# A graph layer with counted slots: longer runs of tiles with a slot range per tile, and row masks by fours

## The chip, the core and the metric

The kernel runs on one core of one Trainium2 chip. Time is device time in microseconds (us) of a whole execution. The engines are PE (matrix products), DVE (VectorE), ACT (ScalarE), POOL (GpSimd) and SP (queues of transfers); each has its own instruction list and they meet at semaphores.

## The reference

Features of 3125 nodes are normalised. 100,000 edges (src, dst, relation), sorted by dst, take the message of their source node, which is a two-layer network with the weights of the edge's relation; the messages are summed by dst. A gated unit and three small layers follow, then a routed feed-forward part for the best half of the nodes. dst is drawn as 3125 u², so low nodes have many more edges.

```
msgs = where(rel == r, relu(relu(S @ W[r].T + b[r]) @ W[r].T + b[r]))   # S = feat[src]
agg = segment_sum(msgs, dst)
gates = agg @ W_ih.T + b_ih + b_hh;  i, f, g, o = split(gates)
hn = sigmoid(o) * tanh(sigmoid(i) * tanh(g))
x = x + (relu(relu(hn @ W1.T + b1) @ W2.T + b2) @ W3.T + b3)
n = layernorm(x);  w = n @ wr + br
x = x + n + (w is among the best half of the nodes) * w * (gelu(n @ f1 + fb1) @ f2 + fb2)
```

## The kernel before

**Table.** Messages depend on source and relation alone, so 2 x 25 blocks of 128 messages are made once (L1109, L1120, `add_bias`, `low`), kept as f16 pairs of 2 x 256 in T and stored in DRAM as message_table. Until about 122 us this is nearly all that runs. Between these steps DVE turns the edge lists, and `make_windows` (L1445) builds the bounds of the tiles: for each tile the lowest node of its window (win_low) and, in slot_row, the node of every slot. POOL fills small constants first (L868 to L897); L897 writes the limits LOWS, HIGHS and SPANS as memsets over columns that share a value.

**The start.** The first thing on DVE's list is `ln(0)`: bn_stats and bn_aggr for four blocks of x, then ve = variance + eps (L1404, a tensor_scalar of 4 columns), ACT's square root, a reciprocal, the scaled features (L1408), and PE's transposes.

**Hot edges.** Edges fall into 782 tiles of 128. The first 393 tiles (TH) hold the nodes below 768 (HOT = 6 blocks). They are counted, not gathered. A window (WINS) is a run of 1 to 16 tiles with at most WIDE = 10 slots, each a node; 152 windows fill 10 blocks (NK) of 128 slots. For each tile DVE makes a mask of source rows (`rows`, L1651, 128 columns, four tiles a step) and one of slot and source block (`key`, L1641, slots x 50 columns), and PE multiplies the two into a bank (`count`, L1304). ACT evicts each finished window into counts (`evict`, L1014). When a block of slots is full, PE multiplies it with the table T: 50 matmuls of 512 columns (`dense`, L1317) in 12 pieces. Then choosing masks spread the slots over the nodes (L1164 for the first four blocks of nodes, "fifth", L1172, for two more).

**Cold edges.** The other 400 tiles are gathered from message_table by POOL, one indirect transfer each (L941), four to a quad, into a ring of 8 quads. A quad's slot is reused when PE has visited it: `visit`, L1336, one matmul a tile with a mask of L1686. Every 4, later every 7 quads (PAUSES) POOL waits for a landing and writes 12 small memsets (L933). The gathers start when the table is stored.

**Dense part.** Seven groups of node blocks (supers 0 to 6) go through aggT (the aggregate, L1187), gates, W1 to W3, n2T, F1 and down (L1150, L1208, L1233); an aggregate needs the visits of all its spans.

**Order.** PE's order is fixed while the program is built: `schedule` plays through all steps with estimated times and takes tiles, dense pieces, quad visits (chunks) and the dense part as they come due; `other_orders` derives the orders of DVE and ACT. DVE, ACT and PE each run strictly in their order.

## Time and profile before

| | us |
|---|---|
| median of 3 runs | 799.16 (797.22 to 802.53) |
| span of the profiled execution | 796.5 |
| PE busy (matmuls) | 703.9, 88% |
| DVE busy | 437.6, 55% |
| POOL busy | 417.8, 52% |
| ACT busy | 243.2, 31% |
| gathers (L941) | 400, 991 ns each |

The profile's numbers are from one execution. A row of a timeline gives the start, the duration, the engine, the line and the operation with its output and inputs; "x8" are eight merged instructions, and the brackets hold the idle time before them and what ended it. A row by stage gives busy time and the number of instructions for each engine, the granted clock of PE as a share, and the DMA's share. Matmuls overlap, so one of them is recorded longer than the distance to the next.

### The profile page before, as it was taken

What the parts mean: (1) busy time and instruction counts of PE and PEld (TensorE: products, weight loads), DVE (VectorE), ACT (ScalarE), POOL (GpSimd) and SP (SyncE); (2) the same over time, 40 slices, a digit from 0 to 9 for tenths busy, and PEclk for the clock granted to TensorE, in tenths of its full rate; (3) what the DMA queues carried; (4) which work ended last, traced back from release to release, by engine and by line L of the source; (5) the groups of instructions that cost most, each with busy time, mean ns of one, the idle gap of its engine ahead of it and who ended that gap; (6) DMA issues with size and microseconds to landing.
All of it is one profiled execution on the core that took longest, in us unless ns stands there. A gap on an engine that the chain in (4) does not pass through costs nothing.

```text
span 796.5 us, 9071 instructions
## 1 busy us (share of the span) xinstructions
PE 703.9 (88%) x2919; PEld 428.7 (54%) x2919; DVE 437.6 (55%) x1566; ACT 243.2 (31%) x418; POOL 417.8 (52%) x773
## 2 busy tenths in 40 slices
PE   2989994769799999889995799999999999699986
PEld 1676683225445555445652356566656556267655
DVE  6849779997988877660321504316026316114375
ACT  1343441121333333344031242332333133131701
POOL 6000004676767766776667677747327677762000
PEclk9999996589999999999997799999999999889999
DMA  9210213323333323333543333323113333331004
GB/s 273 73 58 12 96 63 104 91 86 93 96 90 87 93 74 93 102 87 96 191 133 92 90 105 90 100 66 93 47 46 93 93 93 92 102 92 45 1 1 161
DMA packets 39368, 71.67 MB, mean 90 GB/s; under 512 B 8448, under 2 KB 25873, under 8 KB 39313
## 3 DMA queue, kind: packets, MB, share of 16 engines
q0 software_dynamic: 19200, 52.45, 23.0%
q1 hardware_dynamic: 19296, 17.77, 7.0%
q10 hardware_dynamic: 816, 0.79, 0.3%
q8 instruction: 25, 0.41, 0.2%
q14 instruction: 31, 0.25, 0.1%
HBM read 61.23 MB, written 9.75 MB: 89 GB/s over the span
## 4 chain that ended last, share of the span: by engine, by line
PE 62%; DVE 14%; POOL 12%; issue 6%; DMA 3%; ACT 2%; SPq 0%; DVEq 0%; POOLq 0%
PE BIG L1150 19%; POOL ring L941 12%; PE SM L1233 10%; PE AG L1336 6%; PE SM L1317 6%; PE BIG L1109 6%; DVE oh_row L1651 4%; DVE oh_key L1641 3%; PE SM L1120 3%; DMA ring<-message_table,rowT 3%; PE AG L1120 3%; PE BIG L1187 2%; PE BIG L1304 2%; PE BIG L1090 2%; PE SM L1208 2%
## 5 line engine op out<-in xcount | busy, mean ns | idle before, releaser
L941 POOL DMA_INDIRECT ring<-message_table,rowT x400 | 396.2, 991 | 267.6 <-DMA message_table<-late 115.7
L1336 PE MATMUL AG<-ring,onehot 128*128 128x512 f16 x400 | 104.7, 394 | 23.2 <-DMA ring<-message_table,rowT 22.6
L1233 PE MATMUL SM<-half_b,late 128*128 128x256 f32 x400 | 94.0, 382 | 0.9 <-ACT late L1060 0.6
L1233 PEld LDWEIGHTS SM<-half_b,late 128*128 128x128 f32 x400 | 74.4, 190 | 18.4 <-issue 5.7
L1336 PEld LDWEIGHTS AG<-ring,onehot 128*128 128x128 f16 x400 | 44.3, 116 | 70.6 <-DMA ring<-message_table,rowT 21.8
L1150 PE MATMUL BIG<-fT,half_a 128*128 128x512 f32 (+1 forms) x192 | 81.8, 581 | 0.0
L1651 DVE TENSOR_SCALAR oh_row<-iota,lists 128x128 f16<-128x128 f16 x393 | 76.0, 270 | 5.9 <-PE BIG L1304 5.8
L1304 PE MATMUL BIG<-oh_key,oh_row 128*128 128x500 f16 (+8 forms) x225 | 61.3, 361 | 19.4 <-DVE oh_row L1651 18.1
L1641 DVE TENSOR_SCALAR oh_key<-iota,lists 128x500 f16<-128x500 f16 (+8 forms) x225 | 64.1, 334 | 19.2 <-PE BIG L1304 18.9
L1150 PE MATMUL BIG<-half_b,half_a 128*128 128x512 f32 (+2 forms) x200 | 73.0, 521 | 0.5 <-ACT half_b L1030 0.5
L1553 DVE TENSOR_TENSOR late<-late 128x1024 f32<-128x1024 f32 (+2 forms) x7 | 7.8, 1111 | 115.1 <-ACT late L1037 115.1
L1014 ACT ACTIVATE half_a<-BIG 128x500 f16<-128x500 f32 (+8 forms) x79 | 39.0, 502 | 103.2 <-PE BIG L1304 101.3
L1686 DVE TENSOR_TENSOR onehot<-dst,iota_b 128x512 f16<-128x512 f16 (+3 forms) x118 | 46.2, 413 | 34.3 <-PE AG L1336 33.2
L1317 PE MATMUL SM<-late,half_a 128*128 128x512 f16 x250 | 63.6, 380 | 0.6 <-ACT half_b L1017 0.5
L1317 PE MATMUL SM<-late,half_b 128*128 128x512 f16 x250 | 61.9, 379 | 0.1
L1014 ACT ACTIVATE half_b<-BIG 128x500 f16<-128x500 f32 (+5 forms) x73 | 36.6, 524 | 75.4 <-PE BIG L1304 75.0
L1150 PEld LDWEIGHTS BIG<-fT,half_a 128*128 128x128 f32 x192 | 36.9, 193 | 40.5 <-issue 36.7
L1060 ACT ACTIVATE late<-BIG,fb 128x512 f32<-128x512 f32 (+2 forms) x56 | 35.6, 642 | 69.0 <-PE BIG L1150 69.0
L1150 PEld LDWEIGHTS BIG<-half_b,half_a 128*128 128x128 f32 x200 | 37.8, 190 | 31.6 <-issue 26.3
L1317 PEld LDWEIGHTS SM<-late,half_a 128*128 128x128 f16 x250 | 34.9, 141 | 21.5 <-ACT half_b L1017 1.4
L1109 PE MATMUL BIG<-fT,WR 128*128 128x512 f32 (+2 forms) x112 | 45.7, 563 | 0.8 <-ACT fT L965 0.8
L1317 PEld LDWEIGHTS SM<-late,half_b 128*128 128x128 f16 x250 | 34.9, 141 | 19.9 <-ACT half_b L1014 0.9
(197 smaller groups left out, 827.9 us busy)
## 6 DMA issues: line engine op xcount, KB each, us to landing
ring<-message_table,rowT POOLq DMA_INDIRECT x400, 2.8
message_table<-late SPq DMA_DIRECT2D x10, 512.0 KB, 3.5
out<-X SPq DMA_DIRECT2D x24, 128.0 KB
X<-in_x SPq DMA_DIRECT2D x4, 512.0 KB, 6.5
half_a<-in_f SPq DMA_DIRECT2D x1, 1024.0 KB, 5.1
half_b<-in_f SPq DMA_DIRECT2D x1, 1024.0 KB, 10.9
message_table<-late SPq DMA_DIRECT2D x2, 384.0 KB, 2.9
half_a<-in_w_ih_t SPq DMA_DIRECT2D x1, 768.0 KB, 4.5
```

The costliest lines, as they stand in the source:

```text
L941: nc.gpsimd.indirect_dma_start(ring[:, to * W:(to + 1) * W], None, table, bass.IndirectOffsetOnAxis(ap=rowT[:, t:t + 1], axis=0)).then_inc ...
L1014: last = nc.scalar.activation(counts(lo // P)[:, lo % P:lo % P + cut - lo, :], b[:, 0:(cut - lo) * A].rearrange("p (n a) -> p n a", a=A), ...
L1109: last = nc.tensor.matmul(b[:, 0:n], WR[:, r, k, m * P:(m + 1) * P], fT[:, k, 0:n], start=(k == 0), stop=(k == KC - 1))
L1120: last = nc.tensor.matmul(b[:, r * D:(r + 1) * D], h1T[:, r, k, j * P:(j + 1) * P], WR[:, r, k, :], start=(k == 0), stop=(k == KC - 1))
L1150: last = nc.tensor.matmul(bank[:, 0:n], weight(k), data(k), start=(k == 0), stop=(k == depth - 1))
L1233: last = nc.tensor.matmul(bank, hidden_of(s)[:, c, j * P:(j + 1) * P], F2[:, c, :], start=(c == 0), stop=(c == HC - 1))
L1304: mm = nc.tensor.matmul(b[:, 0:k * A], oh_row[:, (t // 4 % RR) * 4 * P + t % 4 * P:(t // 4 % RR) * 4 * P + (t % 4 + 1) * P], key_slot(t)[: ...
L1317: mm = nc.tensor.matmul(bank[:, :], counts(k)[:, :, a], T[:, a, :], start=(a == 0), stop=(a == A - 1), skip_group_check=True)
L1336: mm = nc.tensor.matmul(AG[w % 2][:, :], hot[:, :, i], ring[:, to:to + W], start=(c == FIRST_OF[w] and i == lo), stop=(c == LAST_OF[w] and ...
L1641: made = nc.vector.tensor_scalar(key_slot(t)[:, 0:k * A], iota16[:, 0:k * A], keyT[:, t:t + 1], None, ALU.is_equal)
L1651: last = nc.vector.tensor_scalar(oh_row[:, to:to + P], iota16[:, 0:P], minus_row[:, 4 * q + i:4 * q + i + 1], 0.0, ALU.add, ALU.is_equal)
L1686: nc.vector.tensor_tensor(onehot[:, (c % OR) * 4 * P:(c % OR + 1) * 4 * P].rearrange("p (n t) -> p n t", t=4)[:, :, lo:hi], dst16[:, t + l ...
```

## The change

- `windows` now forms runs of 4 to 32 tiles in steps of four. Within a run each tile has its own slot range (at most 10 slots), given as an offset to the lowest node of one tile of the run (`offsets`, `OFFSET`, `WIDTH`). 39 runs hold 392 tiles in 8 blocks of slots (NK = 8). `riffled` takes runs from the low half and the high half of the tiles in turn.
- The slots of a run are cut into PARTS of at most 10 slots, one bank each: 121 in place of 152. A tile that crosses a cut has two matmuls: 529 in place of 393. All key masks together have 114,600 columns in place of 151,250.
- `rows` makes the masks of four tiles in one tensor_tensor of 512 columns, with the tile as the inner index; `count` reads every fourth column of it.
- Limits of the tiles are finer (GRAIN = 32 nodes), and widths and offsets stand for each tile: POOL writes LOWS, HIGHS, WIDTHS and OFFSETS, 57 + 56 + 218 + 338 = 669 memsets, in place of 39 + 38 + 34 = 111. They count on a semaphore of their own (bounds_set), for which make_windows waits; the other constants are 13.
- make_windows takes two operations for each of the 39 runs, in place of two for each of 34 groups of windows.
- A dense block is issued in 25 pieces of two matmuls. The step "fifth" is gone: choosing masks are listed by super and the aggregates of supers 0 and 1 read them directly (16 masks; 15 before). Homes of sums, the conditions on them and the planner's durations follow. The weights for the gates are loaded after the 7th dense block, the others after the 8th.

```diff
-    NK = 10
+    NK = 8
     WIDE = 10
+    GRAIN = 32
+    SLOT_PRICE = 0.09
...
-    TH = end_tile(HOT - 1)
+    TH = 4 * round(end_tile(HOT - 1) / 4)
...
-        best = {TH: (0.0, 0, 0)}
-        for t in range(TH - 1, -1, -1):
+        best = {TH: (0.0, 0, 0, [])}
+        for t in range(TH - 4, -1, -4):
             ways = []
-            for m in range(1, min(16, TH - t) + 1):
-                k = slots_for(t, m)
-                if k <= WIDE:
-                    ways.append((best[t + m][0] + k * (0.084 + 0.0209 * m) + 0.3, m, k))
-            best[t] = min(ways)
+            for c in range(t, min(TH, t + 16)):
+                made = [offsets(c, i) for i in range(t - c, 0)]
+                for e in range(c, min(TH, t + 32)):
+                    made = made + [offsets(c, e - c)]
+                    if max(b - a for a, b in made) > WIDE:
+                        break
+                    slots = max(b for _, b in made) - min(a for a, _ in made)
+                    if (e + 1) % 4 == 0 and slots <= P:
+                        cost = sum(max(0.06, (b - a) * A / 2400 + 0.03) for a, b in made) + slots * SLOT_PRICE
+                        ways.append((best[e + 1][0] + cost, e + 1, c, made))
+            best[t] = min(ways, key=lambda way: way[0])
...
-    WINS = windows()
+    WINS = riffled(widened(windows()))
...
-    N_CONSTS = 14 + len(LOWS) + len(HIGHS) + len(SPANS)
+    OFFSETS = segments(lambda t: OFFSET[t], TH)
+    WIDTHS = segments(lambda t: WIDTH[t], TH)
+    N_CONSTS = 13
+    N_BOUNDS = len(LOWS) + len(HIGHS) + len(OFFSETS) + len(WIDTHS)
...
-        PIECES = 12
+        PIECES = 25
...
-            for t, made in ((low_t, LOWS), (high_t, HIGHS), (span_t, SPANS)):
+            for t, made in ((low_t, LOWS), (high_t, HIGHS), (width_t, WIDTHS), (tile_low, OFFSETS)):
                 for lo, hi, v in made:
-                    nc.gpsimd.memset(t[:, lo:hi], float(v)).then_inc(consts, 1)
+                    nc.gpsimd.memset(t[:, lo:hi], float(v)).then_inc(bounds_set, 1)
...
+                rows = oh_row[:, (n // 4 % RR) * 4 * P:(n // 4 % RR + 1) * 4 * P].rearrange("p (n t) -> p n t", t=4)
+                for p, lo, hi in HALVES[n]:
+                    at_slot = PARTS[p][0]
+                    mm = nc.tensor.matmul(BIG[at[("big", "window", p)] % 4][:, (lo - at_slot) * A:(hi - at_slot) * A],
+                                          rows[:, :, n % 4], key_slot(n)[:, (lo - first) * A:(hi - first) * A],
+                                          start=(n == FIRST_IN[p]), stop=(n == LAST_IN[p]), skip_group_check=True)
...
+                dve.wait_ge(bounds_set, N_BOUNDS)
                 dve.wait_ge(big_free, at[("big", "spread", 3)] + 1)
-                for t, m, k, n, slot in RUNS:
...
+                for j, (t, c, nodes) in enumerate(WINS):
+                    first, k, m = min(a for a, _ in nodes), slots_of(nodes), len(nodes)
+                    nc.vector.tensor_scalar(slot_row[:, SLOT0[j]:SLOT0[j] + k], iota16[:, 0:k], tmin_b[:, c:c + 1], float(first),
+                                            ALU.add, ALU.add)
+                    last = nc.vector.tensor_scalar(tile_low[:, t:t + m], tile_low[:, t:t + m], tmin_b[:, c:c + 1], None, ALU.add)
...
-                for i in range(min(4, TH - 4 * q)):
-                    to = (q % RR) * 4 * P + i * P
-                    last = nc.vector.tensor_scalar(oh_row[:, to:to + P], iota16[:, 0:P], minus_row[:, 4 * q + i:4 * q + i + 1], 0.0,
-                                                   ALU.add, ALU.is_equal)
-                last.then_inc(rows_made, 1)
+                t, to = TILES[4 * q][0], (q % RR) * 4 * P
+                nc.vector.tensor_tensor(oh_row[:, to:to + 4 * P].rearrange("p (n t) -> p n t", t=4),
+                                        row16[:, t:t + 4].unsqueeze(1).broadcast_to([P, P, 4]),
+                                        iota16[:, 0:4 * P].rearrange("p (n t) -> p n t", t=4), ALU.is_equal).then_inc(rows_made, 1)
```

On POOL the last constants and the first gathers, before (half_a holds the limits, ring the gathered rows):

```order
L897 MEMSET half_a 128x40 x2
L897 MEMSET half_a 128x9
L897 MEMSET half_a 128x1
L897 MEMSET half_a 128x27
L900 TENSOR_LOAD plan
L900 ISA x2
L941 DMA ring<-message_table,rowT 128x512 x16
```

The same place now (half_b holds the offsets; these are the last of 338):

```order
L971 MEMSET half_b 128x1 x11
L971 MEMSET half_b 128x2
L971 MEMSET half_b 128x1 x17
L971 MEMSET half_b 128x2
L971 MEMSET half_b 128x1 x10
L971 MEMSET half_b 128x2
L971 MEMSET half_b 128x1 x260
L974 TENSOR_LOAD plan
L974 ISA x2
L1015 DMA ring<-message_table,rowT 128x512 x12
```

The run of memsets ahead of the gathers is longer by 558 instructions, most of them one column wide.

On DVE in the first third of the hot phase, before (oh_row: row masks; oh_key, half_b, half_a and late: places of key masks):

```order
L1641 TENSOR_SCALAR oh_key<-iota,lists 128x200 x4
L1651 TENSOR_SCALAR oh_row<-iota,lists 128x128 x4
L1641 TENSOR_SCALAR oh_key<-iota,lists 128x200 x2
L1641 TENSOR_SCALAR half_b<-iota,lists 128x200 x2
L1651 TENSOR_SCALAR oh_row<-iota,lists 128x128 x4
```

And now:

```order
L1700 TENSOR_TENSOR oh_row<-row,iota 128x512
L1691 TENSOR_SCALAR late<-iota,lists 128x400
L1691 TENSOR_SCALAR late<-iota,lists 128x500
L1700 TENSOR_TENSOR oh_row<-row,iota 128x512
L1691 TENSOR_SCALAR oh_key<-iota,lists 128x400
L1691 TENSOR_SCALAR oh_key<-iota,lists 128x350
L1691 TENSOR_SCALAR oh_key<-iota,lists 128x250 x2
```

Four row masks became one instruction, and narrow and wide keys stand mixed.

On PE while the second dense block is due, before (BIG: banks of counts, SM: the dense block's bank, AG: sums of gathered rows):

```order
L1317 MATMUL SM<-late,half_b 128x512 x4
L1336 MATMUL AG<-ring,onehot 128x512 x4
L1304 MATMUL BIG<-oh_key,oh_row 128x300
L1317 MATMUL SM<-late,half_b 128x512 x4
L1304 MATMUL BIG<-oh_key,oh_row 128x300
```

And now:

```order
L1384 MATMUL AG<-ring,onehot 128x512 x4
L1352 MATMUL BIG<-oh_key,oh_row 128x100 x2
L1365 MATMUL SM<-late,half_b 128x512 x2
L1352 MATMUL BIG<-oh_key,oh_row 128x150 x2
L1365 MATMUL SM<-late,half_b 128x512 x2
```

Dense matmuls now stand in twos between tiles. The first dense block is due after 76 tiles (138 before); 35 quad visits (49 before) stand ahead of the aggregate of super 0. From the aggregate of super 4 to the end PE's steps are the same.

## Rows read from the trace of the kernel before

**Rows 1.** The page's chain that ended last: shares of the span by engine.

```profile
PE 62%; DVE 14%; POOL 12%; issue 6%; DMA 3%; ACT 2%; SPq 0%; DVEq 0%; POOLq 0%
```

**Rows 2.** Busy time by stage: PE, PEld, DVE, ACT, POOL, PE's clock, DMA, GB/s.

```profile
122.00:180.00 58.00, 35.39 (x153) 14.52 (x152) 56.82 (x290) 10.46 (x26) 37.17 (x59) 0.68 0.30 87
180.00:392.00 212.00, 196.38 (x914) 109.82 (x912) 146.08 (x610) 67.34 (x134) 149.22 (x254) 1.00 0.33 94
392.00:632.00 240.00, 224.86 (x812) 132.34 (x813) 76.24 (x196) 73.83 (x101) 152.65 (x227) 0.96 0.32 94
```

**Rows 3.** Timeline of POOL: start, us, then instruction; idle before it and releaser.

```profile
128.59 1.12 POOL L941 DMA_INDIRECT ring<-message_table,rowT  x1 [115.67 <-DMA message_table<-late]
...
492.40 0.45 POOL L933 MEMSET pause_out<- 128x4 f32 x12 [1.83 <-DMA ring<-message_table,rowT]
...
530.61 0.45 POOL L933 MEMSET pause_out<- 128x4 f32 x12 [1.84 <-DMA ring<-message_table,rowT]
...
538.38 0.95 POOL L941 DMA_INDIRECT ring<-message_table,rowT  x1 [7.32 <-PE AG L1336]
...
574.70 0.94 POOL L941 DMA_INDIRECT ring<-message_table,rowT  x1 [11.08 <-PE AG L1336]
...
591.04 1.00 POOL L941 DMA_INDIRECT ring<-message_table,rowT  x1 [11.66 <-PE AG L1336]
...
624.19 0.94 POOL L941 DMA_INDIRECT ring<-message_table,rowT  x1 [0.74 <-PE AG L1336]
...
722.66 0.95 POOL L941 DMA_INDIRECT ring<-message_table,rowT  x1 [0.30 <-issue]
```

**Rows 4.** Timeline of PE, same columns.

```profile
73.43 2.29 PE L1144 MATMUL BIG<-ident,half_a 128*128 128x1 f32 x20
...
380.68 10.96 PE L1317 MATMUL SM<-late,half_b 128*128 128x512 f16 x50
...
622.89 7.07 PE L1336 MATMUL AG<-ring,onehot 128*128 128x512 f16 x32
631.57 1.05 PE L1336 MATMUL AG<-ring,onehot 128*128 128x512 f16 x4 [1.61 <-DMA ring<-message_table,rowT]
...
697.99 1.90 PE L1336 MATMUL AG<-ring,onehot 128*128 128x512 f16 x4 [2.81 <-DMA ring<-message_table,rowT]
```

**Rows 5.** Groups of DVE: busy us, mean ns of one, idle before.

```profile
L1651 DVE TENSOR_SCALAR oh_row<-iota,lists 128x128 f16<-128x128 f16 x393 | 76.0, 270 | 5.9 <-PE BIG L1304 5.8
L1641 DVE TENSOR_SCALAR oh_key<-iota,lists 128x500 f16<-128x500 f16 (+8 forms) x225 | 64.1, 334 | 19.2 <-PE BIG L1304 18.9
...
L1686 DVE TENSOR_TENSOR onehot<-dst,iota_b 128x512 f16<-128x512 f16 x30 | 12.5, 418 | 0.1
```

**Rows 6.** Timeline of DVE up to the windows' bounds.

```profile
8.47 4.48 DVE L1404 TENSOR_SCALAR ve<-mv 128x4 f32<-128x4 f32 x1
...
17.52 0.17 DVE L1404 TENSOR_SCALAR ve<-mv 128x4 f32<-128x4 f32 x1
...
59.50 0.16 DVE L1450 TENSOR_TENSOR half_a<-ring,iota 128x2 f32<-128x2 f32 x1 [4.55 <-ACT half_b L999]
...
65.94 0.57 DVE L1459 TENSOR_TENSOR half_a<-half_a,half_b 128x393 f32<-128x393 f32 x1
```

**Rows 7.** The memsets of L897: timeline of POOL, and one group by form.

```profile
7.38 5.55 POOL L897 MEMSET half_a<- 128x163 f32 x111
...
L897 POOL MEMSET half_a<- 128x12 f32 x17 | 1.1, 98 | 0.0
```

**Rows 8.** Busy time of L897 in half microseconds: POOL (x starts), clock, DMA.

```profile
9.50:10.00 0.50, 0.50 (x7) 1.00 1.19 290
12.00:12.50 0.50, 0.50 (x15) 1.00 1.08 327
```

**Rows 9.** Busy time of the gathers (L941) by stage: POOL, clock, DMA.

```profile
128.00:300.00 172.00, 118.67 (x117) 0.90 0.31 89
300.00:460.00 160.00, 109.14 (x113) 0.94 0.37 111
```

421 lines of the change are left out of this document (218 added, 203 removed).

## Prediction

> **What bounds the kernel now.** I read the chain of waits first. PE holds 62% of it, but GpSimd's row gathers (POOL, L941) are its second largest entry [rows 1], so two things take turns. The busy time by stage shows how. From 122 to 180 us VectorE is busy 56.8 of 58 us and PE waits for masks at a granted clock of 0.68; from 180 to 392 PE is busy 196 of 212 us with the rest of the hot phase; from 392 to 632 it is busy 225 of 240 us with the first four supers of the dense part [rows 2].
>
> Then POOL's timeline. 400 gathers start at 128.59 and at 722.66 us. As long as nobody holds them they keep their own pace: from the pause at 492.40 to the one at 530.61, 28 gathers and a pause take 38.2 us. Four times a gather finds its ring slot unread, released by PE's visits (L1336): 7.32, 11.08, 11.66 and 0.74 us, all between 531 and 625 us [rows 3]. Beyond the 0.30 us that stands before any gather this is 30.8 - 1.2 = 29.6 us. So the gathers run free until 531 us, are then held up because PE is late, and PE is late because the hot phase ended at 392.
>
> PE's timeline closes the argument: at 631.57 and 697.99 us PE itself waits for a gather (the latter feeds the aggregate of super 5). From 697.99 to the end PE works through an order that waits little, 98.5 us [rows 4]. The end is thus set by "start of the gathers + their own pace + what PE holds them up + 98.5 us". With the 29.6 us gone the last two visits move to 602.0 and 668.4 us, if PE is there by then.
>
> **The change, part by part.**
>
> *PE in the hot phase.* Dense blocks go from 10 to 8, so from 500 to 400 matmuls of 512 columns; 50 take 10.96 us, 0.219 each [rows 4]: -21.9 us. Tile matmuls go from 151,250 columns in 393 to 114,600 in 529; at the same 0.428 ns a column 64.8 against 49.1 us, and I add 3 us for 122 pieces of 50 or 100 columns, whose cost no row shows at full clock: -13 us. Ahead of the first aggregate 35 quad visits stand instead of 49; 32 matmuls of a visit take 7.07 us [rows 4], so 14 visits of 4 are 12.4 us, which leave this phase but are done later.
>
> *VectorE in the hot phase.* 393 row masks (76.0 us busy) become 98 compares of 512 elements. The quad mask of L1686 is the same shape and operand pattern: 418 ns. 98 x 0.418 = 41 us. Keys cost 0.285 us each now (64.1 us for 225), and get narrower: at most 112 us [rows 5]. With 30 quad masks and the sums some 170 us, below PE's need, so VectorE limits only the start, where no dense block is due: 76 tiles now, 138 before.
>
> *Where the hot phase then ends.* 52 + 88 + 35 x 4 x 0.221 (31) = 171 us of PE work, and the first 76 tiles at the old pace at worst (58 us for 138, so 32 us, less their 9 us of matmuls): 122 + 4 + 171 + 23 = 320 us instead of 392. The dense part up to the aggregate of super 4 takes 240 us as now [rows 2], with 12.4 us of visits deferred into it: 572 us. The gather for it lands at 602. PE has 30 us to spare, so the hold-ups of the gathers go: **-29.6 us**. The other 40 us that the hot phase gains buy nothing; PE will stand waiting for gathers. From the aggregate of super 4 on, PE's order is the same step for step, so the last 98.5 us stay. Cover: if PE were later by more than 30 us, the excess comes back.
>
> *Memsets on POOL.* Slot ranges for each tile turn 111 constant memsets into 669 (57 + 56 bounds, 218 widths, 338 offsets). POOL itself has nothing to do until 128 us, and their reader, make_windows, starts at 59.50 us [rows 6]: free at first sight. But look at VectorE at 8.47 us: a tensor_scalar of four elements (ve, L1404) takes 4.48 us, where the same line takes 0.17 at 17.52 [rows 6]. It ends at 12.95. POOL's run of 111 memsets begins at 7.38 and lasts 5.55, to 12.93 [rows 7]. I read this as VectorE being shut out for the whole run of memsets, and everything hangs on it: ve goes to the square root, to the first transposes and through the whole message table, so to the start of the gathers.
>
> How long is the new run? Narrow memsets start 15 in 0.5 us, so every 0.033 us; wide ones 7 in 0.5 us [rows 8]; the mean of the old run is 0.050. The 113 bounds at 0.045 are 5.1 us, 556 narrow ones at 0.033 are 18.3: 23.4 us. One iota less stands ahead, so it runs from 7.2 to 30.6 us. The release of ve moves from 12.95 to 30.6: **+17.7 us**. Bounds: 0 (not shut out) and, at the old mean for all 669, 33.5 us, so 40.7, +27.8. I take the value for narrow ones, since the 556 are 1 to 17 wide, nearly all 1 to 4.
>
> The Trainium skill (SBUF — State Buffer, "Who interferes with whom") says that a tensor_scalar in a 2-port mode and a GpSimd instruction exclude each other for one whole instruction. That agrees on who blocks whom. Read to the letter, a wait would end with the memset then running, within 0.1 us; by that the sum would be 17.7 us lower. The row shows 4.48 us, through some 90 memsets, and I go by the row; the letter is a rival below.
>
> *make_windows.* 34 pairs of operations take 59.50 to 65.94 us [rows 6]; 39 pairs at the same 0.19 us would end 1 us later, and they lose the wide ones. The slot matmuls on PE that read them start at 73.43 [rows 4]: 0, with 7 us of cover. These matmuls go from 20 to 16 at 0.115 us: **-0.4 us**, on PE's path to the table.
>
> *Gathers beside masks.* 117 gathers from 128 to 300 us are busy 118.67 us, 1.014 each; 113 from 300 to 460 us 109.14, 0.966 each [rows 9]. The difference goes with VectorE's density of mask instructions. These go from 2 a tile to 1.25, and the phase is shorter: between 0 and -5 us, I take **-2 us**.
>
> *The rest* (buffers placed elsewhere, no "fifth" step, 16 choosing masks for 15, weight loads with the 7th and 8th block) lies inside PE's 30 us, at the tail nowhere: 0. That the runs don't fit the data, so that the general loops start, I exclude: worked out from the drawn edges, every tile stays inside its range.
>
> Sum: 796.5 + 17.7 - 29.6 - 0.4 - 2 = 782.2 us for the profiled execution. Its span of 796.5 is 2.7 us under the median of the runs, 799.16. Predicted: 782.2 + 2.7 = **785 us**.
>
> **The rivals.**
>
> *A: no shutting out.* VectorE gets in between two memsets, and the 4.48 us have another cause. For it: this is a single case, and two ends 0.02 us apart can be chance. Against it: the same line without memsets beside it takes 0.17 us, and no transfer or semaphore stands before it. Time: 785 - 17.7 = 767. Chance 0.12. The Trainium skill's page named above, to the letter, gives this case.
>
> *B: the run of memsets is longer*, at 0.050 us each, or the instruction ahead of ve (ident, L1378) is caught too: 785 + 10 = 795, no change to speak of. 0.15.
>
> *C, slower: the memsets start every 0.098 us*, which is what a narrow one is recorded with [rows 7], since 669 in one run may not be fed as fast as 111. Then the run ends at 7.2 + 65.6 = 72.8, the release moves by 59.8 us: 767 + 60 = 827. It turns to slower by over 1% from about 0.068 us a memset. Against it: 15 in 0.5 us. 0.05.
>
> *D: PE is late all the same*, because 121 evictions, the clock or narrow matmuls stretch the hot phase by over 30 us and half the hold-ups return: 785 + 15 = 800. Against it: PE is at full clock from 180 us on and has 30 us. 0.03.
>
> **How the numbers follow.** The sum as it stands, with a run of 18 to 28 us and 0 to -5 from the gathers: 778 to 790, chance 0.60. The last 0.05 is for things I have not thought of, spread on all sides. About 1% is what a measurement can tell from no change, 8 us here. Faster by over 1% (under 791.2): 0.60 + A 0.12 + 0.03 = 0.75. Within 1%: B, D and 0.01: 0.19. Slower: C and 0.01: 0.06. The range from 766 to 798 takes in A and B.
>
> **What would show it.** In the trace after: ve of super 0 ends with the last memset, near 30.6 us, and at 17 us of shift the first gather starts near 146; POOL has no wait for PE above 1 us; PE stands idle for gathers between 400 and 680 us; the hot phase lasts under 200 us; the last wait for a gather before the end lies 98.5 us from it. The prediction is wrong if ve takes 0.2 us (A), if the first gather starts after 155 (B, C), or if POOL still waits for PE (D).

## The result, and the profile after

The changed kernel takes 807.07 us (median of 4 runs, 803.59 to 810.34), the kernel before 799.12 in the same runs: a ratio of 1.0098, with a 95% interval of 1.0056 to 1.0140. Forecast were 785 us and a range of 766 to 798. On a second chip 10 runs gave 804.52 us against 800.09, a ratio of 1.0082 [1.0049, 1.0115]. The change makes the kernel about 1% slower.

The profiled execution took 803.59 us with a span of 801.7, 5.2 more than before. Four points on the clock split these 5.2 us. Times are in us from the span's start.

| point | before | after | shift |
|---|---|---|---|
| PE's first transposes | 14.96 | 33.17 | +18.2 |
| first gather | 128.59 | 154.11 | +25.5 |
| last gather | 722.66 | 727.79 | +5.1 |
| end | 796.5 | 801.7 | +5.2 |

So the start is 25.5 us later, the stretch from the first to the last gather 20.4 us shorter (573.7 for 594.1), and the tail the same to 0.1 us. The forecast had +17.3, -31.6 and 0.

The start, in the timeline of VectorE of the changed kernel (start, duration, instruction; in brackets the idle time before it and what ended it). L1452 is ve, which was L1404, and L1456 the scaling:

```profile
8.98 9.72 DVE L1452 TENSOR_SCALAR ve<-mv 128x4 f32<-128x4 f32 x1
18.98 0.18 DVE L1454 RECIPROCAL rs<-sd 128x4 f32<-128x4 f32 x1 [0.27 <-ACT sd L1033]
19.19 13.83 DVE L1456 TENSOR_SCALAR agg_ring<-X,mv,rs 128x256 f32<-128x256 f32 x4
```

And the 669 memsets in the timeline of POOL:

```profile
7.15 11.52 POOL L971 MEMSET half_a<- 128x83 f32 x297
19.23 1.21 POOL L971 MEMSET half_a<- 128x1 f32 x34 [0.55 <-issue]
20.37 11.54 POOL L971 MEMSET half_b<- 128x12 f32 x338
```

The run ends at 31.9 us (forecast 30.6). It has one break, 0.55 us wide, from 18.68 to 19.23. ve ends in it, at 18.70, after 9.72 us. The scaling then comes at 19.19, as the memsets go on, and its four operations, 0.4 us each otherwise, end at 33.0. Before, ve took 4.48 us beside 111 memsets that lasted 5.55 us [rows 6, 7].

The second part of the late start stands in PE's timeline:

```profile
91.93 1.84 PE L1215 MATMUL BIG<-ident,half_a 128*128 128x1 f32 x16
93.64 5.40 PE L1180 MATMUL BIG<-fT,WR 128*128 128x512 f32 x12
104.33 3.59 PE L1180 MATMUL BIG<-fT,WR 128*128 128x512 f32 x4 [5.30 <-ACT slot_node L1077]
```

The slot matmuls are 18.5 us later than before (91.93 for 73.43, [rows 4]), which is the hold. Then PE waits 5.30 us for the eviction of the slots, and its next four matmuls take 3.59 us where twelve took 5.40: 1.8 us too long. The windows of the same stretch show a granted clock of 1.00 while PE idles and 0.57 just after it, about the lower of its two levels (1.2 for 2.4 GHz):

```profile
99.00:104.00 5.00, 0.03 (x1) 0.00 (x0) 4.70 (x14) 1.26 (x2) 0.00 (x0) 1.00 0.29 97
104.00:108.00 4.00, 3.67 (x7) 1.65 (x8) 3.65 (x13) 2.05 (x6) 0.00 (x0) 0.57 0.41 141
```

The gathers, in POOL's timeline: the first, the only two that PE held, and the last.

```profile
154.11 1.37 POOL L1015 DMA_INDIRECT ring<-message_table,rowT  x1 [122.19 <-DMA message_table<-late]
...
478.48 0.94 POOL L1015 DMA_INDIRECT ring<-message_table,rowT  x1 [6.36 <-PE AG L1384]
...
510.77 1.08 POOL L1015 DMA_INDIRECT ring<-message_table,rowT  x1 [5.01 <-PE AG L1384]
...
727.79 0.94 POOL L1015 DMA_INDIRECT ring<-message_table,rowT  x1 [0.30 <-issue]
```

Beyond the usual 0.30 us these are 10.8 us, where before stood 29.6 [rows 3] and 0 was forecast. The sum of PE's waits (total, times, longest, in us) shows the other side:

```profile
PE AG L1384 <- DMA ring<-message_table,rowT: 63.6, 22, 5.4
PE BIG L1161 <- DVE agg_ring L1456: 33.2, 1, 33.2
PE BIG L1352 <- DVE oh_row L1700: 7.9, 10, 4.2
PE BIG L1180 <- ACT slot_node L1077: 5.3, 1, 5.3
```

PE now waits 63.6 us for gathers, and the page's chain of waits reads so:

```profile
PE 36%; POOL 35%; issue 16%; DVE 7%; DMA 5%; ACT 1%; SPq 0%; POOLq 0%; DVEq 0%
```

PE falls from 62% [rows 1] to 36%, and the gathers take its place.

### The profile page after: what moved, and what is told of

Read it like the earlier page. It is cut to its first block, busy times and chain, and to the rows that moved or that the text cites. A ratio compares the mean times of both kernels' runs of the same rounds, so it can differ in the third digit from the quotient of the medians.

```text
span 801.7 us, 9441 instructions
## 1 busy us (share of the span) xinstructions
PE 670.9 (84%) x2965; PEld 424.5 (53%) x2965; DVE 417.4 (52%) x1280; ACT 226.0 (28%) x386; POOL 434.1 (54%) x1330
## 4 chain that ended last, share of the span: by engine, by line
PE 36%; POOL 35%; issue 16%; DVE 7%; DMA 5%; ACT 1%; SPq 0%; POOLq 0%; DVEq 0%
POOL ring L1015 34%; PE BIG L1221 12%; PE SM L1290 7%; PE BIG L1180 4%; DMA ring<-message_table,rowT 3%; PE AG L1384 3%; PE SM L1191 2%; PE AG L1191 2%; PE BIG L1244 2%; PE BIG L1161 1%; DVE ve L1452 1%; POOL pause_out L1007 1%; DMA X<-in_x 1%; DVE half_a L1499 1%; DVE half_b L1501 1%
## 5 line engine op out<-in xcount | busy, mean ns | idle before, releaser
L1015 POOL DMA_INDIRECT ring<-message_table,rowT x400 | 393.7, 984 | 255.2 <-DMA message_table<-late 122.2
L1384 PE MATMUL AG<-ring,onehot 128*128 128x512 f16 x400 | 112.9, 419 | 63.6 <-DMA ring<-message_table,rowT 63.6
L1290 PE MATMUL SM<-half_b,late 128*128 128x256 f32 x400 | 94.1, 383 | 0.9 <-ACT late L1131 0.6
L1290 PEld LDWEIGHTS SM<-half_b,late 128*128 128x128 f32 x400 | 74.3, 190 | 18.1 <-issue 5.7
L1365 PE MATMUL SM<-late,half_a 128*128 128x512 f16 x200 | 59.1, 381 | 0.3 <-ACT half_b L1090 0.3
L1691 DVE TENSOR_SCALAR oh_key<-iota,lists 128x350 f16<-128x350 f16 (+8 forms) x224 | 56.1, 306 | 4.9 <-PE BIG L1352 4.6
L1352 PE MATMUL BIG<-oh_key,oh_row 128*128 128x250 f16 (+9 forms) x299 | 52.7, 271 | 6.6 <-DVE oh_row L1700 6.4
L1365 PE MATMUL SM<-late,half_b 128*128 128x512 f16 x200 | 55.4, 381 | 1.1 <-ACT half_b L1087 0.7
L1352 PEld LDWEIGHTS BIG<-oh_key,oh_row 128*128 128x128 f16 x299 | 30.5, 115 | 29.5 <-DVE oh_row L1700 8.7
L1700 DVE TENSOR_TENSOR oh_row<-row,iota 128x512 f16<-128x512 f16 x98 | 40.7, 416 | 9.5 <-PE BIG L1352 9.5
L1087 ACT ACTIVATE half_a<-BIG 128x500 f16<-128x500 f32 (+9 forms) x61 | 29.5, 508 | 55.0 <-PE BIG L1352 50.9
L1103 ACT ACTIVATE half_b<-BIG 128x512 f32<-128x512 f32 (+2 forms) x14 | 7.7, 551 | 131.0 <-PE BIG L1244 131.0
L1087 ACT ACTIVATE half_b<-BIG 128x500 f16<-128x500 f32 (+8 forms) x60 | 29.9, 519 | 52.0 <-PE BIG L1352 47.9
```

The lines of the kernel that those rows point to most:

```text
L1015: nc.gpsimd.indirect_dma_start(ring[:, to * W:(to + 1) * W], None, table, bass.IndirectOffsetOnAxis(ap=rowT[:, t:t + 1], axis=0)).then_inc ...
L1087: last = nc.scalar.activation(counts(lo // P)[:, lo % P:lo % P + mid - lo, :], b[:, 0:(mid - lo) * A].rearrange("p (n a) -> p n a", a=A), ...
L1290: last = nc.tensor.matmul(bank, hidden_of(s)[:, c, j * P:(j + 1) * P], F2[:, c, :], start=(c == 0), stop=(c == HC - 1))
L1352: mm = nc.tensor.matmul(BIG[at[("big", "window", p)] % 4][:, (lo - at_slot) * A:(hi - at_slot) * A], rows[:, :, n % 4], key_slot(n)[:, (lo ...
L1365: mm = nc.tensor.matmul(bank[:, :], counts(k)[:, :, a], T[:, a, :], start=(a == 0), stop=(a == A - 1), skip_group_check=True)
L1384: mm = nc.tensor.matmul(AG[w % 2][:, :], hot[:, :, i], ring[:, to:to + W], start=(c == FIRST_OF[w] and i == lo), stop=(c == LAST_OF[w] and ...
```

## Experiments

"Calm" is a chip on which the kernel before takes 800 us. Four of the eighteen runs (e0, e5, e6, e8) were on a calm one. The fourteen others fell on four chips where the kernel before takes 897 to 913 us, those with "calm" in their names too, which were given before the chip was known. There ACT, VectorE and PE wait in the middle of the kernel, 10 to 76 us at a time, for something that the profile doesn't name (last section), so times there are compared only with the kernel before on the same chip. The start, up to the first gather, shows no such waits (the changed kernel: 154.1 us calm, 154.4 not), and is read from any chip. Ratios are to the kernel before on the same chip.

### The memsets and VectorE

**e1_sets_spread and, once more, e10_sets_spread_again.** The memsets in four runs:

```
+ if n == 24: pool.wait_ge(diag_ready, 1)
+ if n == 224: pool.wait_ge(feat_ready, 3)
+ if n == 554: pool.wait_ge(feat_ready, 4)
  nc.gpsimd.memset(t[:, lo:hi], float(v)).then_inc(bounds_set, 1)
```

> The changed kernel with the same 669 memsets, in four runs: 24 at the start, 200 behind VectorE's diagonal lists, 330 behind its scaling of super 2, 115 behind that of super 3. In these stretches VectorE, in the trace after, waits for PE or runs the tensor_tensor and scalar_tensor_tensor lines of the table. Theory (VectorE's tensor_scalars of super 0 are shut out for as long as the memsets run without a break; 18.2 us of the shift of the table): ve takes under 1.5 us, PE's first transposes start at 11 to 15 us instead of 33.2, the first gather near 135 us instead of 154.1, and the time falls by 17 to 22 us from the changed kernel's 807, to 785 to 790 or up to 3 us lower since before had 4.3 us of hold too. Rival (the memsets are not the cause, the start is late for another reason): no change, 807. Second rival (the operations of those stretches are held too, so the hold only moves): the first gather stays at 150 or later and the time above 800.

> The changed kernel with the memsets in four runs beside VectorE's waits, once more, for a chip on which the kernel before takes 800 us. Theory (the hold of VectorE at the start is worth what its first gather shows, 18 to 20 us against the trace in which the whole run held it, some 14 against one where VectorE got in at the gap): first transposes at 11 us, first gather at 133 to 136 us, the wait for slot_node stays at 5.3 us; 785 to 791 us, which is 0.98 to 0.99 of the kernel before. Rival (later waits take it back, since the gathers are then held more often): above 795.

First transposes at 10.9 and 11.2 us, first gather at 134.25 and 134.57: 19.7 us earlier than in the changed kernel, as expected; the wait for slot_node stays at 5.30. The first transposes are also 4 us earlier than before, since that kernel's hold of 4.48 us [rows 6] is gone too. Both fell on a chip with stalls: 899.71 us, ratio 0.9875 [0.9784, 0.9967], and 913.66 us, ratio 1.0002 [0.9946, 1.0058]. The place of the delay and its size up to the first gather are shown; the expected times could not be read.

**e2_sets_in_pieces.** The memsets stay where they are, with a break after every 32:

```
+ if n and n % 32 == 0:
+     pool.wait_ge(bounds_set, n)
  nc.gpsimd.memset(t[:, lo:hi], float(v)).then_inc(bounds_set, 1)
```

> The changed kernel with the memsets where they are, but after every 32 of them GpSimd waits until they have all been counted. In the trace after, ve was let in at a single gap of 0.55 us in the run, after 297 memsets. Theory (VectorE is let in at the first gap, however short, and is held for a run, not for memsets as such): each held tensor_scalar waits 1.2 us at most (32 at 0.037), ve ends before 11 us, the four of the scaling take under 6 us together, PE's first transposes start at 13 to 20 us and the time falls by 13 to 19 us from 807. Rival (what counts is how much GpSimd writes in that time, not the breaks): ve still ends behind most of the memsets, and the time stays within 3 us of 807.

VectorE's timeline of this run:

```profile
9.26 0.72 DVE L1454 TENSOR_SCALAR ve<-mv 128x4 f32<-128x4 f32 x1
10.26 0.18 DVE L1456 RECIPROCAL rs<-sd 128x4 f32<-128x4 f32 x1 [0.27 <-ACT sd L1035]
10.47 3.15 DVE L1458 TENSOR_SCALAR agg_ring<-X,mv,rs 128x256 f32<-128x256 f32 x4
```

ve takes 0.72 us for 9.72, the scaling 3.15 for 13.83, and PE begins at 13.76, though as many memsets stand there and they last to 34.5 us. The first gather is at 141.63. The breaks are short: the memsets on both sides of one start 0.16 us apart, for 0.034 otherwise, which leaves POOL idle for 0.06 us. So VectorE is held until the next break, not for the amount written. The time on this chip is 911.91 us, ratio 0.9964 [0.9909, 1.0020].

**e5_before_more_sets.** The kernel before with 558 more memsets:

```
+ for n in range(558):
+     nc.gpsimd.memset(half_b[:, 2048 + TW + TH + n:2048 + TW + TH + n + 1], 0.0).then_inc(consts, 1)
```

> The kernel before with 558 further memsets of one column behind its 111, each written to a place of its own that nobody reads; nothing else is changed. Theory (the run alone makes the shift): the run lasts from 7.4 to about 32.5 us, ve or the scaling behind it ends with it, PE's first transposes start at 32 to 34 us instead of 15.0, the first gather near 147 us, and the time rises by 17 to 19 us over the kernel before (2.2%). Rival (only the changed kernel's other edits make the start late): ve takes 4 to 5 us as before, time within 3 us.

Calm chip: 816.63 us, ratio 1.0204 [1.0138, 1.0270], 16.5 us more (17 to 19 expected). But the start came out otherwise than expected. PE's first transposes are at 21.05, not at 32 to 34, and the first gather is at 142.66. VectorE and POOL:

```profile
8.93 10.11 DVE L1406 TENSOR_SCALAR ve<-mv 128x4 f32<-128x4 f32 x1
...
19.53 1.38 DVE L1410 TENSOR_SCALAR agg_ring<-X,mv,rs 128x256 f32<-128x256 f32 x4
```

```profile
12.87 6.15 POOL L899 MEMSET half_b<- 128x1 f32 x185
19.73 12.70 POOL L899 MEMSET half_b<- 128x1 f32 x373 [0.71 <-issue]
```

Here the break is 0.71 us wide and the memsets go on at 19.73, 0.20 after the scaling has begun. This time the scaling runs through in its usual 1.38 us. The rest of the hold falls on the ve of super 1, 8.85 us from 23.61. Of the 16.6 us between the spans, 14.1 stand at the first gather and 2.5 behind it. The memsets alone make the kernel slower, and how much depends on what gets through at the break.

**e0_changed_again.** The changed kernel, unchanged.

> The changed kernel itself, as the reference of the other runs of this chip. The four runs before this one were on a chip where the kernel before took 909 us, not 799, with stalls of up to 38 us on PE and 54 us on VectorE in the stretch of the gathers. Theory (the stalls belong to that chip; the order of the two kernels is set by what the first traces show): where the kernel before takes 797 to 803 us, this takes 804 to 811. Rival (on a chip with the stalls the difference is another one): there the two differ by more than 1.5%, in either direction.

Calm chip: 804.52 us (797.83 to 811.13, 10 runs), ratio 1.0082 [1.0049, 1.0115]. The profiled execution is the fastest of the ten (the nine others take 804.1 to 811.1), and in it the scaling gets through at the break, as in e5:

```profile
19.20 1.38 DVE L1456 TENSOR_SCALAR agg_ring<-X,mv,rs 128x256 f32<-128x256 f32 x4
```

```profile
19.40 1.63 POOL L971 MEMSET half_a<- 128x1 f32 x34 [0.71 <-issue]
```

The scaling starts 0.01 us later than in the first trace, the memsets 0.17 us later, and now the 34 memsets take 1.63 us for 1.21: POOL is the one that waits. PE begins at 20.72, 12.4 us earlier, but the last 338 memsets then hold the ve of super 1:

```profile
23.28 9.15 DVE L1452 TENSOR_SCALAR ve<-mv 128x4 f32<-128x4 f32 x1
```

The first gather is at 148.18, 5.9 us before that of the first trace; the span is 795.9 us. So the start of this kernel scatters by some 6 us with what happens at one break. Of the ten traces with this run of memsets unbroken (the changed kernel, e0, e3, e4, e8, e11, e13, e15, e16, e17), two, e0 and e15, have the early start.

### VectorE's work between supers 1 and 4

**e3_check_later.** make_windows in two, the tiles and the check of the ranges directly ahead of make_keys:

```
  if s == LISTS_AT + 1:
+     check_windows()
      make_keys()
```

> The changed kernel with make_windows in two: the 39 operations that make the slots stay where they are, the 39 of the tiles and the check of the ranges (10.7 us together) go behind the scaling of super 4, just ahead of make_keys. Theory (the 5.3 us that PE waits at 104 us hang on VectorE: the eviction of the slots on ACT stands behind the square root of super 4, which waits for ve, which waits for make_windows; the change made that 4.6 us longer and there was no cover; 1.8 us more go to the clock after the wait): the wait of L1180 vanishes, the first gather starts 6 to 8 us earlier (146 to 148), and the time falls by 6 to 8 us, to 799 to 801. Rival (the slots themselves are late, their matmuls or what they read): the wait stays at 3 us or more and the time falls by less than 3 us.

A miss. The wait for slot_node vanishes, but this takes its place, on PE:

```profile
126.94 1.54 PE L1161 MATMUL BIG<-ident,agg_ring 128*128 128x128 f32 x6 [9.92 <-DVE agg_ring L1456]
```

First gather at 161.37, 7 us later than in the changed kernel instead of 7 earlier; 925.67 us, ratio 1.0116 [1.0033, 1.0199], on a chip with stalls. VectorE had 12.3 us more in super 2, which with make_keys and the biases made 18 us. Both readings of mine were too narrow. What bounds there is VectorE's whole work in a super, and not the place of one eviction; the next run tests this.

**e7_vector_spread (and e12_vector_spread_calm, the same kernel).** The memsets as in e1, and the slots behind super 1, the tiles behind super 2, the check behind super 3, make_keys behind super 4:

```
  if s == LISTS_AT + 1:
+     place_tiles()
+ if s == LISTS_AT + 2:
+     check_windows()
+ if s == LISTS_AT + 3:
      make_keys()
```

> The same, and make_windows cut into the slots, the tiles and the check, one super each, make_keys behind them; the planner's costs as they were. In the first try of this cut, with both later parts and the keys in one super, the 5.3 us of waiting for slot_node became 9.9 us of waiting for the features of super 5, since VectorE had 18 us of work more in that super. Theory (7 us of the late start are VectorE's work between supers 1 and 4): first gather at 125.5 to 128 us, 7 to 9 us ahead of the run with the memsets alone, and the time lower by as much, 777 to 783. Rival (the planner's costs did it in the run with all three): within 3 us of the run with the memsets alone.

First gather at 126.09 us, 8.3 ahead of the memsets alone (134.4), and no wait of PE above 1.2 us is left between the lists and the table's end. That confirms the size and the place. The time, on a chip with stalls: 899.67 us, ratio 0.9907 [0.9860, 0.9954]. The second time:

> The changed kernel with the memsets in four runs and VectorE's work cut up, the planner's costs as they were. Where the kernel before takes 800 us: first gather at 126 us. Theory one (the holds are worth their 8.6 us): holds of 10 to 12 us as in the changed kernel, first to last gather 574 to 582 us, 775 to 783 us. Theory two (fewer holds only mean slower gathers and longer pauses): first to last gather 571 to 575, 772 to 776 us, no different from the run with the new costs, 773.8.

Another chip with stalls: first gather at 126.98, 912.38 us, ratio 0.9900 [0.9840, 0.9961].

### Everything together

**e6_all_three.** e7 and the planner's costs as the trace has them:

```
- {"aggT": 0.3, "gates": 1.4, "W1": 0.24, "W2": 0.12, "W3": 0.24, "n2T": 0.25, "F1": 0.24}
+ {"aggT": 0.3, "gates": 2.6, "W1": 0.47, "W2": 0.25, "W3": 0.5, "n2T": 0.26, "F1": 0.435}
- return 0.24 * len(down_parts(s[0])[s[2]])
+ return 0.45 * len(down_parts(s[0])[s[2]])
- now += 0.06 + 0.24 * (hi - lo)
+ now += 0.02 + 0.215 * (hi - lo)
- hot_at = max(hot_at, now - 5.0) + 0.27 + ...
+ hot_at = max(hot_at, now - 5.0) + 0.2 + ...
```

> The changed kernel with the memsets in four runs beside VectorE's waits, with make_windows cut into the slots (super 1), the tiles (super 2) and the check (super 3), make_keys behind super 4, and with the planner's costs as measured. On the first chip's base of 807. Theory (all three delays are apart and on the path): first transposes near 11 us, no wait for slot_node or for VectorE's features above 1 us up to the end of the table, first gather at 125 to 130 us, holds on GpSimd under 3 us, last gather 9 to 14 us earlier counted from the first: 20 + 7 + 11 = 38 us less, 764 to 775. Rival (PE's order or the tail takes the gain of the new plan back): first gather as said, but 776 to 790. On a chip with the long stalls the start is as said and the time follows the stalls; the difference to the changed kernel there is 15 to 45 us.

Calm chip: **773.77 us**, ratio 0.9663 [0.9610, 0.9717]. It beats the kernel before by 3.4% and the changed kernel beside it by 3.8% (804.52), inside the 764 to 775 us expected. First transposes at 11.07, first gather at 125.86, last at 699.09:

```profile
125.86 1.62 POOL L1021 DMA_INDIRECT ring<-message_table,rowT  x1 [69.96 <-DMA message_table<-late]
...
444.63 0.94 POOL L1021 DMA_INDIRECT ring<-message_table,rowT  x1 [3.08 <-PE AG L1390]
```

The holds fell to 2.8 us, as expected. Yet from first to last gather it is 573.2 us, as in the changed kernel, and not 9 to 14 us less: the gain from the holds doesn't appear in the sum. Where, the calm chips show, in us:

| | before | after | e0 | e6 | e8 |
|---|---|---|---|---|---|
| first to last gather | 594.1 | 573.7 | 573.7 | 573.2 | 578.3 |
| held by PE | 29.6 | 10.8 | 9.6 | 2.8 | 8.2 |
| 400 gathers busy | 396.2 | 393.7 | 394.8 | 399.6 | 397.2 |
| idle ahead of the pauses | 37.7 | 38.3 | 38.3 | 39.8 | 42.5 |

From e0 to e6 the holds lose 6.8 us, the gathers gain 4.8 and the pauses 1.5. Half of this loss stands far from any hold: the 51st gather starts 76.0 us behind the first in e6 and 72.7 in e0, and PE holds none of these in either kernel. From there to the last gather e6 needs 497.2 us and e0 501.0, 3.8 us less with holds shorter by 6.8. Why the first 50 are slower in e6 isn't shown; all three edits are in it. The gain of e6 over the changed kernel is thus nearly all at the start (22.3 of 23.7 us between the two spans); what the new costs bring can't be told apart in it. The next runs were to show them alone.

**e4_plan_costs, e11_plan_costs_again, e13_plan_costs_calm, e15_plan_costs_third, e16_plan_costs_pair.** The changed kernel with only the costs of e6, five times.

> The changed kernel with the planner's costs as the trace after has them: gates 2.6 us a block for 1.4, W1 0.47 for 0.24, W2 0.25 for 0.12, W3 0.5 for 0.24, a chunk of F1 0.435 for 0.24, a piece of down 0.45 for 0.24, a visit 0.02 + 0.215 a tile for 0.06 + 0.24, and 0.2 for 0.27 us a hot tile. Only the order on PE, VectorE and ACT changes: 33 quad visits instead of 35 stand ahead of the first aggregate. Theory (PE waits 17 us for gathers between 338 and 385 us because the plan puts too many visits there, then falls behind, so that the gathers are held 11.7 us at 478 and 511 us): the holds on GpSimd fall under 3 us, the last gather moves 9 to 14 us earlier, and the time falls by as much, to 793 to 798. Rival (the holds come from the depth of the ring and the bulk of the work between visits, whatever the order): holds of 8 us or more, time within 4 us of 807. Second rival (the new order costs as much at the end, where the plan before fitted): the last gather earlier, the tail behind it longer than 83.5 us by as much.

> The changed kernel with nothing but the planner's costs as measured, once more. From the run with all three edits, whose holds on GpSimd fell from 11.4 to 2.8 us while first to last gather took 573.2 us as against 573.7. Theory one (the new order is worth the holds less what the denser gathers cost): holds under 4 us, first to last gather 569 to 574, time 3 to 5 us below the changed kernel, 800 to 803. Theory two (the holds only become slower gathers and pauses, so the order is worth nothing): time within 2 us of the changed kernel's 804 to 807. Rival (the new order by itself is worth the whole 8 us): 796 to 799.

> The changed kernel with the planner's costs alone. Theory one: holds under 4 us, first to last gather 565 to 571 us, 796 to 801 us. Theory two: holds under 4 us, gathers busy 398 us or more for 394, first to last gather 572 to 575, within 2 us of the changed kernel's 804 to 807.

> The changed kernel with the planner's costs alone, where the kernel before takes 800 us. Theory one (the holds are worth their length): holds under 4 us, first to last gather 565 to 571 us, 796 to 801 us. Theory two (fewer holds only mean slower gathers and longer pauses, as the run with all three edits suggests): holds under 4 us, gathers busy 398 us or more, first to last gather 572 to 575, within 2 us of the changed kernel's 804 to 807.

> The changed kernel with the planner's costs alone. Calm chip (kernel before at 800 us), theory one: first to last gather 565 to 571 us, 796 to 801 us; theory two: 572 to 575 us, within 2 us of the changed kernel. Chip with stalls (kernel before near 900 us): 1.01 to 1.03 of the kernel before, as in two runs so far; if the order is what loses there, more than 1% above the changed kernel beside it, and if not, within 1% of it.

All five fell on chips with stalls: 928.86, 926.12, 927.02, 921.13 and 927.57 us, ratios of 1.0184 [1.0113, 1.0255], 1.0109 [1.0018, 1.0199], 1.0141 [1.0076, 1.0205], 1.027 by the medians alone for the fourth (896.67 before), and 1.0170 [1.0096, 1.0244]. Beside the last ran **e17_changed_pair**:

> The changed kernel. Calm chip: 804 to 808 us, 1.005 to 1.012 of the kernel before. Chip with stalls: the late start is there in full (first gather 148 to 154), so 1.01 to 1.02 of the kernel before; if it is above 1.02 or below 1.00, the stalls fall differently in the two kernels and set the result there.

It took 935.50 us (919.14 to 938.26), with 909.80 of the kernel before beside it: by the medians 1.028, without an interval, since the runs scatter too much. With one run at 919 and three above 935 the pair doesn't tell which of the two is better. What the order alone is worth on a calm chip stays open.

### The row masks

**e8_rows_apart.** The changed kernel with the masks made one tile at a time again:

```
- nc.vector.tensor_tensor(... row16 ... iota16 ..., ALU.is_equal)
+ for i in range(4):
+     nc.vector.tensor_scalar(oh_row[...i...], iota16[:, 0:P], minus_row[:, t + i:t + i + 1], 0.0, ALU.add, ALU.is_equal)
```

> The changed kernel with the row masks made one tile at a time again (four tensor_scalars of 128 elements a quad, 0.19 us each, for one compare of 512, 0.42), all else the same. Theory (the hot phase has 17 us of waiting for gathers behind it, so what the masks gain buys nothing): PE's hot phase gets 5 to 20 us longer, the waits for gathers behind it as much shorter, the first gather and the holds on GpSimd stay within 3 us, and the time within 5 us of the changed kernel. Rival (the masks are worth what they take off VectorE): the time rises by 10 us or more.

Two groups of VectorE (count, busy us and mean ns of one), the first of the changed kernel, the second of e8:

```profile
L1700 DVE TENSOR_TENSOR oh_row<-row,iota 128x512 f16<-128x512 f16 x98 | 40.7, 416 | 9.5 <-PE BIG L1352 9.5
```

```profile
L1698 DVE TENSOR_SCALAR oh_row<-iota,minus_row 128x128 f16<-128x128 f16 x392 | 77.8, 276 | 1.3 <-PE BIG L1352 1.3
```

37.1 us of VectorE's time (the compare takes 416 ns, forecast 418), and the first aggregate stands at 341.2 us for 330.9, 10.3 later with the same first gather (154.07) as in the changed kernel's first trace. The time: 807.85 us, ratio 1.0103 [1.0041, 1.0164], 3.3 above the changed kernel beside it, which is no difference by the intervals, and within the 5 us expected. Between the two traces with the same first gather, the last gather is 4.6 us apart (732.41 for 727.79). So the compare does what was forecast of it, and over half of the 10.3 us that it gains on PE are waited away again.

### Fewer pauses

**e9_longer_bursts, e14_longer_bursts_calm.** e6 with pauses every 7 quads from the start.

```
- PAUSES = [4 * i for i in range(1, FIRST_BURSTS + 1)]   # FIRST_BURSTS 14
+ PAUSES = [7 * i for i in range(1, FIRST_BURSTS + 1)]   # FIRST_BURSTS 1
```

> The kernel with all three edits, and the gathers' pauses every 7 quads from the start (14 pauses) for every 4 quads in the first 56 (20 pauses). A pause costs 3.1 us: 28 gathers and one take 38.2. Theory (from the first gather on the kernel is bound by the chain of gathers and pauses): first to last gather 573 - 6 x 3.1 = 554 us if PE follows; PE then has less slack and holds gathers again for 3 to 8 us: 757 to 765 us. Rival (the pauses let something through that the engines need, as the stalls of 20 to 76 us on ACT, VectorE and PE suggest which stood in the traces of the slower chip and ended behind pauses): engines that wait for no semaphore for more than 5 us between 130 and 400 us, and 774 or more.

> All three edits and 14 pauses instead of 20. Theory (chain of gathers and pauses is the bound): first to last gather 552 to 560 us, PE's waits for gathers fall from 60 us to 40 to 50, 755 to 765 us. Rival (PE cannot follow): holds of 10 us or more come back, time above 768.

On chips with stalls both: 897.31 us, ratio 0.9875 [0.9835, 0.9916], and 899.82, ratio 0.9797 [0.9731, 0.9863]. The second was faster than e12 and e13 on the same chip, but from first to last gather it is 687 to 691 us there, so the chain of the gathers is not what binds on these chips, and the expected 755 to 765 could not be looked for.

## Why the prediction was wrong

**What bounds.** Right: "start of the gathers + their own pace + what PE holds them up + 98.5 us" describes before, after and e6. PE's last wait for a gather is at 703.08, 98.6 us ahead of the end, and last gather to end is 73.8, 73.9 and 73.1 us. That first step carried everything else.

**Memsets, +17.7.** Right in mechanism, and 18.2 in the profiled execution. The run took 24.8 us for the forecast 23.4, the run ended at 31.9 for 30.6. Not foreseen was the break in it, which makes the price scatter: 33.2 or 20.7 us for the first transposes, 154.1 or 148.2 for the first gather. Rival A falls with e2 and e5. The Trainium skill (SBUF — State Buffer, "Who interferes with whom") says "Whoever issues first gets the shared pair for the whole instruction". That one of the two waits for the other agrees with the traces (POOL 1.63 us for 1.21 in e0, VectorE 12.87 us for one operation in the first trace); who was first they don't show, since VectorE's held operation is recorded as begun up to 0.13 us before the memset. Read as a wait of one instruction it doesn't agree: 9.72 us stand there for ve, through the whole unbroken run, and 0.72 in pieces of 32.

**make_windows, 0: the first step that failed**, by 7 us. "0, with 7 us of cover" had two errors. First the price: 78 tensor_scalars that read a scalar from memory start every 0.14 us, where the 68 tensor_tensors and copies started every 0.095 [rows 6]. The pairs take from 78.08 to 88.97 us, 10.9 for 6.4. I had written "39 pairs at the same 0.19 us", though the diff shows another kind of operation. Then the cover: I compared the end of make_windows with PE's slot matmuls. But what was late next was VectorE itself. Behind make_windows it has the sums of super 2 and ve of super 4, ACT's square root waits for that ve, and the eviction of the slots stands behind the square root. These are the lines of ACT, before and after:

```profile
80.48 0.20 ACT L959 ACTIVATE sd<-ve 128x4 f32<-128x4 f32 x1 [3.10 <-DVE ve L1404]
80.59 0.16 ACT L1003 ACTIVATE slot_node<-BIG 128x10 f32<-128x10 f32 x1
```

```profile
104.00 0.20 ACT L1033 ACTIVATE sd<-ve 128x4 f32<-128x4 f32 x1 [3.10 <-DVE ve L1452]
104.12 0.16 ACT L1077 ACTIVATE slot_node<-BIG 128x8 f32<-128x8 f32 x1
```

Before, the eviction ended at 80.8 us, just as PE needed its bank: its 16 matmuls from 75.58 took 7.21 us there, and 7.03 in the other supers. The cover was 0, not 7. The 4.5 us became 5.3 of waiting, and the lower clock after it cost 1.8 more. The 0.4 us for fewer slot matmuls was right.

**Holds, -29.6: the second step that failed**, by 11 us. "PE has 30 us to spare" was right where I looked, at the aggregate of super 4: there PE waits eight times for a gather, from 599 to 637 us. The hot phase ended in time too (331 us, 179 after its start, forecast under 200; of the forecast's excess 4.4 us are visits, since the 35 have 120 matmuls by the trace and not 140). But the spare time was not to be had at one point for all. In PE's timeline behind the first aggregate:

```profile
338.75 1.03 PE L1384 MATMUL AG<-ring,onehot 128*128 128x512 f16 x4 [1.32 <-DMA ring<-message_table,rowT]
341.44 1.06 PE L1384 MATMUL AG<-ring,onehot 128*128 128x512 f16 x4 [1.67 <-DMA ring<-message_table,rowT]
342.34 10.46 PE L1221 MATMUL BIG<-half_b,half_a 128*128 128x512 f32 x24
...
359.66 1.90 PE L1384 MATMUL AG<-ring,onehot 128*128 128x512 f16 x4 [4.62 <-DMA ring<-message_table,rowT]
364.62 1.90 PE L1384 MATMUL AG<-ring,onehot 128*128 128x512 f16 x4 [3.06 <-DMA ring<-message_table,rowT]
```

PE stands here for eight visits, 17.3 us in all up to 382, because its order is fixed and the plan had put them there for a hot phase that it thought 17 us longer (195.7 us from the first tile to the first aggregate by the planner's own costs, 179 in the trace). Then it works from 386 to 517 us without a wait for a gather, one super in 54 us where the plan had 41, and in this stretch the gathers find their slots unread, at 478 and 511. So -18.8 instead of -29.6. That the plan's misjudgement causes the holds is supported by e6, where with its costs corrected 2.8 us are left, but not isolated: e6 has the two other edits as well, and neither e7 nor the costs alone ran on a calm chip. What the holds cost the kernel isn't measured either: past the first 50 gathers e6 has 6.8 us less of them and is 3.8 us shorter.

**Gathers, -2.** Busy time fell by 2.5 us: right here.

**The order of the errors.** 796.5 + 18.2 + 0.3 + 6.6 + 0.4 - 18.8 - 2.5 + 0.6 + 0.4 = 801.7: the hold, PE's first matmuls, the slots (5.3 + 1.8 - 0.4, with 0.1 of rounding), the rest of the table, the holds of the gathers, their busy time, the pauses, and what is left over in the chain and the tail. That is 19.5 us above the forecast span of 782.2. The other 2.6 us up to the 807.07 measured lie in the step from the span to the median, forecast 2.7 as before and measured 5.4, since the profiled execution was the fastest of four. The two failed steps are 7 and 11 us, and both had the same form: cover read at one point, for an engine whose lateness shows at another.

## What to carry to other kernels

A "free" step has to be followed to the next thing that the same engine does, and the next, until a wait of before takes up the delay: e3 and e7 differ, besides the memsets, only in where VectorE's tiles, check and keys stand; their first gathers are 35 us apart, 20 of them by the memsets and 15 by this. Long back-to-back runs of small GpSimd instructions belong where VectorE doesn't run tensor_scalars, or need breaks: 20 waits of GpSimd on its own semaphore, with 0.06 us of idle time each, bring VectorE's ve from 9.72 to 0.72 us. Time to spare against a stream such as the gathers holds only at the place in the fixed order at which it was read.

## What the hardware showed that was not expected

**A break decides by tenths of a microsecond.** VectorE's four scaling operations start every 0.33 us, the first at 19.2 (19.5 in e5). Where the memsets resume 0 to 0.07 us behind its start (six traces, the first one with 0.03), it takes about 12.9 us. Where they resume 0.18 to 0.20 us behind it (e0, e5, e15), all four get through in 1.38 us and POOL waits (1.63 us for 34 memsets instead of 1.21). A wider break doesn't help by itself. In e16 it is the widest, 0.86 us, and the memsets resume at 19.54, just behind the start of the second operation:

```profile
19.20 0.41 DVE L1456 TENSOR_SCALAR agg_ring<-X,mv,rs 128x256 f32<-128x256 f32 x1
...
19.52 12.85 DVE L1456 TENSOR_SCALAR agg_ring<-X,mv,rs 128x256 f32<-128x256 f32 x1
```

In e8 (0.13 us behind) the first operation takes 4.62 us and the second 8.60, and where the one ends, at 23.8, that run has a second break of 0.12 us. The long break, 0.51 to 0.86 us after about 300 instructions of the run, is no instruction of the program.

**Some chips stall.** On the six calm traces (before, the changed kernel, e0, e5, e6 and e8) no engine waits over 10 us for something that the profile doesn't name. On the other chips each trace has 6 to 14 such waits, on ACT above all. Their length overstates the stall. This is the line of ACT's waits for the aggregate (total, times, longest) in e4, and below it the same line of the changed kernel on the calm chip:

```profile
ACT half_b L1103 <- remote: 129.7, 7, 76.4
ACT half_b L1103 <- PE BIG L1244: 131.0, 14, 48.3
```

"remote" is a semaphore event to which the profile finds no instruction. Waiting for PE here is thus ordinary, up to 48.3 us; in the 76.4 us of e4 the last of the matmuls that ACT waits for ends at 739.6 and ACT goes on at 770.98, so 31.3 us are the stall. In that time PE has work too, and does it slowly: its matmuls of L1290 start 1.4 to 2.8 us apart from 740.8 to 758.3.

The kernel before is 12 to 14% slower there as well. All of the 46 waits over 27 us had at least one pause of the gathers in them, and 45 ended within 20 us of one. That says less than it seems: of 30 us placed at random between the gathers of a kernel with 20 pauses, 83 to 87% have a pause in them on these chips and 61 to 64% end as close behind one. With fewer pauses (e9, e14) the longest waits were not longer, 46 and 47 us for 76, but there were more over 10 us (14 and 13, for 6 to 12 elsewhere) and the first came at 161 and 169 us, for 215 us at the earliest elsewhere. The cause is open. A kernel judged on one chip should be looked at on a second: e7 and e14 keep a gain of 1 to 2% there, e4 none.
